# Regions of a routed decoder layer cleared early, filler units in other banks, and identity matmuls in the pauses of the last pairs' chain

## The reference

```python
x = layernorm(x + attention(x))            # 16 heads of 64, Wq, Wkv, Wo, bo
x = layernorm(x + mlstm(x, ctx, ctx))      # 4 heads of 64: decay matrix from gates, running maxima, RMS norm
xn = layernorm(x) * gamma + beta           # 8 experts, hidden 1024, the best 2 for each token
p = softmax(xn @ Wr + br); scores, idx = top_k(p, 2)
y_e = relu(xn @ W1[e] + b1[e]) @ W2[e] + b2[e]
x = layernorm(x + sum_k scores[k] * (y[idx[k]] - c[idx[k]] + sum_e c[e]))   # c[e] = relu(b1[e]) @ W2[e] + b2[e]
```

## Time and profile before

| | us |
|---|---|
| median of 3 runs | 877.47 |
| lowest, highest | 872.62, 878.78 |
| the profiled execution | 873.39 |
| its span, first to last instruction | 871.6 |
| pairs and their units (to about 456) | 456 |
| chain of the last pairs (to the first expert tile at 530) | 74 |
| expert tiles (530 to 811) | 281 |
| tail | 61 |

### The profile page before, as it was taken

The page is one execution under the profiler, slowest core; times in us unless marked ns, Lnnn a source line. Parts: engine busy times, 40 slices in busy tenths (PEclk is TensorE's granted clock), DMA queues, the critical chain, the costliest instruction groups (busy, mean ns, idle before and its releaser), DMA issues.

```text
span 871.6 us, 14654 instructions
## 1 busy us (share of the span) xinstructions
PE 709.3 (81%) x4812; PEld 604.3 (69%) x4813; DVE 467.3 (54%) x1078; ACT 328.4 (38%) x987; POOL 246.4 (28%) x196
## 2 busy tenths in 40 slices
PE   5798989988088988989858415999999999998763
PEld 4687877878077868778656314888888888787421
DVE  4334454843255846558465773555555555555345
ACT  4475666746055746646443201222222222222111
POOL 3100010300311302113034347637227300600473
PEclk9899999989589989899785556999999999999755
DMA  9533333331301001010052015615324411110243
GB/s 312 150 116 115 128 116 116 127 115 37 126 14 37 26 19 55 1 38 25 2 181 66 7 42 175 188 61 164 130 66 156 138 36 42 61 37 19 68 122 113
DMA packets 62507, 77.36 MB, mean 89 GB/s; under 512 B 5836, under 2 KB 54520, under 8 KB 62456
## 3 DMA queue, kind: packets, MB, share of 16 engines
q1 hardware_dynamic: 53832, 47.29, 16.9%
q0 software_dynamic: 8608, 29.37, 10.3%
q10 hardware_dynamic: 16, 0.01, 0.0%
HBM read 45.04 MB, written 31.62 MB: 88 GB/s over the span
## 4 chain that ended last, share of the span: by engine, by line
PE 62%; DVE 11%; ACT 11%; POOL 7%; issue 5%; DMA 4%; POOLq 0%; SPq 0%; DVEq 0%; ACTq 0%
PE bank L919 13%; PE bank L693 7%; PE bank L695 6%; PE bank L694 6%; ACT arena L1026 6%; PE bank L889 4%; PE bank L891 4%; PE bank L890 4%; PE bank L899 4%; POOL arena L683 4%; PE bank L838 3%; PE bank L807 3%; DVE arena L1187 2%; PE bank L771 2%; ACT arena L999 1%
## 5 line engine op out<-in xcount | busy, mean ns | idle before, releaser
L919 PE MATMUL bank<-w_ring,hidT_hi 128*128 x320 | 119.9, 408 | 3.3 <-DVE hidT_lo L1535 3.3
L1026 ACT ACTIVATE arena<-bank,negmx 128x128 f32<-128x128 f32 x256 | 90.7, 373 | 51.7 <-DVE negmx L1179 51.5
L1142 ACT ACTIVATE hidT_hi<-bank 128x512 fp32r<-128x512 f32 x80 | 43.5, 596 | 174.6 <-PE bank L899 174.6
L618 POOL DMA_INDIRECT xg_dram<-arena,slot x32 | 34.2, 1067 | 174.8 <-DVE slot L1378 112.0
L919 PE MATMUL bank<-w_ring,hidT_lo 128*128 x320 | 83.4, 281 | 0.0
L1508 DVE TENSOR_TENSOR arena<-bank,b_rep 128x512 f32<-128x512 f32 x80 | 55.3, 691 | 41.9 <-PE bank L891 41.5
L1185 DVE RECIPROCAL rinv<-rsum 128x8 f32<-128x8 f32 x32 | 6.5, 203 | 127.4 <-ACT arena L1026 127.4
L889 PE MATMUL bank<-w_ring,xgT_hi 128*128 x160 | 67.8, 424 | 4.5 <-DVE xgT_lo L1527 2.7
L919 PEld LDWEIGHTS bank<-w_ring,hidT_hi 128*128 128x128 f32 x320 | 60.1, 188 | 15.0 <-issue 4.0
L1514 DVE TENSOR_REDUCE work<-bank 128x256 f32<-128x512 f32 x40 | 27.7, 691 | 79.5 <-PE bank L919 79.5
L574 POOL TENSOR_TENSOR w_ring<-w_raw,w_ring 128x2048 fp32r<-128x2048 f32 x14 | 64.4, 4597 | 1.2
(11 more groups left out here) (240 smaller groups left out, 1839.7 us busy)
## 6 DMA issues: line engine op xcount, KB each, us to landing
xg_dram<-zeros SPq DMA_DIRECT2D x9, 2176.0 KB, 9.1
w_raw<-in_L_ffn_W_dram POOLq DMA_DIRECT2D x16, 1024.0 KB, 5.8
work<-xg_dram SPq DMA_DIRECT2D x40, 128.0 KB, 2.0
y_dram<-work SPq DMA_DIRECT2D x40, 128.0 KB, 1.7
b_rep<-in_L_ffn_b_dram POOLq DMA_DIRECT2D x8, 512.0 KB, 4.1
work<-gmax_dram SPq DMA_DIRECT2D x14, 256.0 KB, 3.7
arena<-in_x_dram SPq DMA_DIRECT2D x8, 256.0 KB, 2.8
xres<-in_x_dram SPq DMA_DIRECT2D x1, 2048.0 KB, 15.1
```

Source lines behind the costliest of these rows:

```text
L919: last = pe.matmul(o, l, r, start=c == 0 and l is both[0], stop=c == FC - 1 and l is both[0])
L1026: last = nc.scalar.activation(probs[:, n % 2, h * S:(h + 1) * S], ps_score[:, h * S:(h + 1) * S], ACT.Exp, bias=negmx[:, n % 2, h:h + 1], ...
```

## The change

Seven edits.

1. Clears: one a step, at steps 1 to 9 of the loop.
2. Banks in the loop: L, R and G go to bank 7 (between two sequences' output projections), T to banks 4 and 5 (between two transposes). Waits on `wo_read`, `pT_copied` and on the readers of T, G and R keep the owners apart.
3. Order in the loop: T first in step 1, G ahead of two v; R in the second list of step 2; S in the first list of step 3. On ACT, `soft_gates` goes to the start of step 2, `exp_of_m` to its end. On DVE, `weigh` goes ahead of the logits, `choose`, `gate_sums` and `head_sums` ahead of `weights_of`, `find_slots` behind it.
4. Bias 0 is loaded ahead of the weights, bias 1 and 2 later.
5. Expert 0 is rounded on ACT ahead of the copy of N(A), its rests are subtracted on DVE within the chain (`rest_early`).
6. Expert 1 is loaded and rounded within the chain (ACT), its first rest is DVE's there, its second GpSimd's after the last scatter (`rest_of_second`).
7. TensorE runs 6 + 22 + 16 + 30 + 16 identity matmuls ahead of five units of the chain and 40 behind it, into bank 6, which nothing reads.

```diff
-        ps_ring = bank[0:6]
+        ps_ring = [*bank[0:6], bank[7]]
...
             if s == 1:
-                return (of("L", i - 3) + of("X", i - 1) + of("x", i + 1) + of("v", i, 1, 0) + of("T", i - 2),
-                        of("v", i, 0, 1) + of("v", i, 1, 1) + of("G", i - 1))
+                return (of("T", i - 2) + of("L", i - 3) + of("X", i - 1) + of("x", i + 1) + of("v", i, 1, 0),
+                        of("G", i - 1) + of("v", i, 0, 1) + of("v", i, 1, 1))
             if s == 2:
-                return (of("U", i - 2, 0) + of("R", i - 3) + of("q", i + 1, 0) + of("U", i - 2, 1) + of("k", i + 1, 0),
-                        of("q", i + 1, 1) + of("k", i + 1, 1))
-            return (of("v", i + 1, 0, 0) + of("w", i, 0, 0) + of("q", i + 1, 2),
-                    of("w", i, 0, 1) + of("k", i + 1, 2) + of("S", i - 1))
+                return (of("U", i - 2, 0) + of("q", i + 1, 0) + of("U", i - 2, 1) + of("k", i + 1, 0),
+                        of("q", i + 1, 1) + of("R", i - 3) + of("k", i + 1, 1))
+            return (of("v", i + 1, 0, 0) + of("S", i - 1) + of("q", i + 1, 2) + of("w", i, 0, 0),
+                    of("w", i, 0, 1) + of("k", i + 1, 2))
...
+                    if not at_end and un[0] in "TLRG":
+                        ks = (4, 5) if un[0] == "T" else (6,)
+                    else:
+                        ks = [(turn + k) % (6 if at_end else 2) for k in range(2 if un[0] in "TB" else 1)]
+                        turn += len(ks)
...
-                    if s < 2 and 2 * i + s <= E:
-                        done(sp, ("q", i, 3) if s == 0 else ("v", i, 1, 1))
-                        clear_rows(2 * i + s)
+                    if 1 <= STEPS * i + s <= E + 1:
+                        done(sp, {0: ("q", i, 3), 1: ("v", i, 1, 1), 2: ("k", i + 1, 1), 3: ("k", i + 1, 2)}[s])
+                        clear_rows(STEPS * i + s - 1)
...
+            def rest_of_second():
+
+                both = w_ring[:, 1, W_WORDS:2 * W_WORDS].rearrange("p (g k n) -> p g k n", k=2, n=D)
+                pool.wait_ge(w_rounded, 4)
+                pool.tensor_tensor(both[:, :, 1, :], w_raw[:, KC * F:2 * KC * F].rearrange("p (g n) -> p g n", n=D),
+                                   both[:, :, 0, :].bitcast(F32), ALU.subtract).then_inc(w_split, 1)
+                pool.wait_ge(w_split, 4)
+                for part in range(2):
+                    load_raw(2, part)
...
                         done(pool, ("v", Z, 1, 1))
+                        load_bias(0)
                         for part in range(2):
                             load_raw(0, part)
-                        load_bias(0)
-            load_bias(1)
             scale_xn(A)
+            rstd_of_pair(Z)
             for b in range(2):
                 mask(Y, b)
-            rstd_of_pair(Z)
-            load_bias(2)
+            load_bias(1)
             scatter(A)
             head_norm(Y)
+            load_after_first(0)
             for b in range(2):
                 mask(Z, b)
             both_norms(Y)
             scale_xn(Y)
+            load_after_first(1)
             head_norm(Z)
             both_norms(Z)
+            load_bias(2)
             scatter(Y)
             scatter(Z)
+            rest_of_second()
             for part in range(2):
-                split_first(part)
-            for e in range(1, RING):
-                for part in range(2):
-                    split(e, part)
+                split(2, part)
...
-            run(DRAIN)
+            def fill(n):
+
+                for _ in range(n):
+                    pe.matmul(bank[6][:, 0:P], ident[:, :], ident[:, :], start=True, stop=True)
+
+            pauses = {("N", A): 6, ("U", Z, 0): 22, ("R", Y): 16, ("N", Z): 30, ("R", Z): 16}
+            for un in DRAIN:
+                fill(pauses.get(un, 0))
+                run([un])
+            fill(40)
...
+                    if s == 2 and i >= 1:
+                        soft_gates(i - 1)
                     copies(before[:early])
...
-                    if s == 3 and i >= 1:
-                        exp_of_m(i - 1)
...
-                    if s == 2 and i >= 1:
-                        soft_gates(i - 1)
                     copies(after[1:])
+                    if s == 2 and i >= 1:
+                        exp_of_m(i - 1)
...
             copy_unit(("C", Z))
-            copy_unit(("N", A))
             act.wait_ge(wo_done, B)
             for part in range(2):
-                round_first(part)
+                round_early(0, part)
+            copy_unit(("N", A))
             copy_unit(("X", Z))
...
             choice_exp(Y)
+            for part in range(2):
+                round_early(1, part)
             copy_unit(("N", Z))
...
+                    if s == 1 and i >= 2:
+                        weigh(i - 2)
                     if s == 1 and i >= 3:
                         logits_in(i - 3)
                     if s == 1 and i + 1 < PAIRS:
                         rest_x(i + 1)
-                    if s == 1 and i >= 2:
-                        weigh(i - 2)
-                    if s == 2 and i >= 3:
-                        find_slots(i - 3)
+                    if s == 1 and i >= 3:
+                        choose(i - 3)
+                    if s == 2 and i >= 1:
+                        gate_sums(i - 1)
+                    if s == 2 and i >= 2:
+                        head_sums(i - 2)
...
                         weights_of(n + 1)
...
                     if s == 1 and i >= 1:
                         read_gates(i - 1)
-                    if s == 2 and i >= 1:
-                        gate_sums(i - 1)
-                    if s == 2 and i >= 2:
-                        head_sums(i - 2)
+                    if s == 2 and i >= 3:
+                        find_slots(i - 3)
...
             weigh(Y)
+            rest_early(0, 0)
             logits_in(A)
...
             both_norms(Y)
+            rest_early(0, 1)
             head_sums(Z)
...
             both_norms(Z)
+            rest_early(1, 0)
             logits_in(Z)
```

More of the change, by code:

```diff
@@ L272, in decoder_layer @@
         proj_done = sem("proj_done")
-        ring_free = [sem(f"ring_free{k}") for k in range(6)]
+        ring_free = [sem(f"ring_free{k}") for k in range(7)]
         scores_done = sem("scores_done")
@@ L392, in decoder_layer @@
         FIRST = [("x", 0), ("q", 0, 0), ("k", 0, 0), ("q", 0, 1), ("k", 0, 1), ("v", 0, 0, 0)]
-        ordinal, place, uses = {}, {}, [0] * 6
-        for banks_of, units in ((2, FIRST + [un for i in range(PAIRS) for s in range(STEPS) for part in fillers(i, s)
-                                             for un in part]), (6, DRAIN)):
+        ordinal, place, uses = {}, {}, [0] * 7
+        for at_end, units in ((False, FIRST + [un for i in range(PAIRS) for s in range(STEPS) for part in fillers(i, s)
+                                               for un in part]), (True, DRAIN)):
             turn = 0
@@ L399, in decoder_layer @@
                     ordinal[un] = len(ordinal)
[L400 to L404 removed]
+                    if not at_end and un[0] in "TLRG":
[3 more added lines that the diff above has]
+                        turn += len(ks)
+                    place[un] = [(k, uses[k]) for k in ks]
+                    for k in ks:
                         uses[k] += 1
@@ L780, in unit @@
                     read(pe, ("N", p))
+                    if p < A:
+                        pe.wait_ge(wo_read, 2 * (p + 3))
                     for b in range(2):
@@ L816, in out_proj @@
                     pe.wait_ge(wo_read, 2 * i + b)
+                if half == 0 and b == 0:
+                    for un in (("G", i - 1), ("R", i - 3)):
+                        if un in place:
+                            read(pe, un)
                 for c in range(4 * half, 4 * half + 4):
@@ L836, in weights_transposed @@
                     pe.wait_ge(pT_copied, n)
+                if n % STEPS == 1 and n // STEPS >= 2:
+                    read(pe, ("T", n // STEPS - 2))
                 for h in range(8):
@@ L1102, in _ @@
                         choice_exp(i - 3)
+                    copies(after[1:])
                     if s == 2 and i >= 1:
-                        soft_gates(i - 1)
-                    copies(after[1:])
+                        exp_of_m(i - 1)
                     act.wait_ge(oT_done, n + 1)
```

33 lines of the change are left out of this document (15 added, 18 removed).

## The result

The changed kernel takes 844.16 us (median of 4 runs, 843.37 to 845.07) beside 875.05 (872.42 to 878.78) of the kernel before on the same chip: a ratio of 0.9644, with a 95% interval of 0.9599 to 0.969. That is 30.9 us less. I had forecast 830, with a range of 818 to 850, so the range held and the forecast was 14 us too low. The narrower range of the forecast itself, 820 to 838, did not hold.

A forecast was written before the change was run, and what follows sets the result against it. TensorE is busy most of the span; bounds are a long wait rooted in SP's queue order, small bank waits, and half clock before the expert tiles. 873.4 - 22.4 - 9.4 - 15.2 = 826.4, plus 4.1 as median: 830; range 818 to 850.

The forecast's parts named there:

- Part 1: Loop: regions of `xg_dram` cleared early, one a step, so the first scatter no longer waits; gain 22.4 us.
- one wait whose root is SP's queue: Long pair, 76.53 us: TensorE waits for VectorE, VectorE for GpSimd, GpSimd for a ninth clear issued late.
- The store of the gate maxima: Pair 1 step 2, behind a clear on SP's queue: lands some 5 us later; up to 1.5 could show, 0 taken.
- Part 2: Loop's order and banks: waits of x, T and R go, a new one comes; gain 9.4 us, bounds 0 and 15.4.
- the new wait: Pairs 3 to 6: U(1) waits for U(0)'s bank, ACT's copy standing behind `soft_gates`; 4.0 us a pair.
- the longer cold stretch: Pairs 3 to 6, behind the idle TensorE of step 2: half clock for longer, may take 0.5 us a pair.
- the new wait eats part 2: Rival, loop: U(1) behind `soft_gates` and a longer low clock leave the reordering worth 0; 840 us, chance 0.17.
- my upper bound: Most that the loop's new order and banks could bring: 15.4 us.
- Part 3: Last pairs' chain up to the first expert tile: bias first, early rests, fills for the clock; gain 15.2 us.
- 0.9 at L(Y): Last pairs' chain: gain at L(Y) from matmuls sped up by fills that raise the clock, capped by VectorE's rests.
- two rests paid for in full: Chain: by the Skill's rule, rests beside GpSimd would cost 4.5 us in place of the 0.5 taken.
- the first two rivals: Loop reordering worth 0 (840 us, chance 0.17); chain gain halved by rests, roundings and falling clock (838 us, chance 0.15).

The follow-up runs named there:

- c1: Kernel before with only the early clears (one region a step, steps 1 to 9): 852.99 us, ratio 0.9728.
- c2: Changed kernel with the loop's order, banks, ACT and VectorE order of before; early clears, chain and fills stay: 841.30 us, ratio 0.9597.
- c8: Changed kernel with 16 identity matmuls ahead of U(1) in pairs 3 to 7, where TensorE waits: 835.71 us, ratio 0.958.
- c10: c5 with, in addition, ACT's copy of q ahead of the exponentials in step 2: 811.87 us, ratio 0.9302.
- c4: Changed kernel with ACT's `soft_gates` behind the copy of U(0) instead of ahead of it: 845.25 us, ratio 0.9647.
- c5: Changed kernel with VectorE's `choose` moved from ahead of the weights in step 1 to behind the maxima in step 2: 819.41 us, ratio 0.9379.
- c12: Changed kernel with `rest_early(0, 1)` moved ahead of the last logits and `rest_early(1, 0)` behind the last slots, load and rounding moved to match: 849.95 us, ratio 0.9742.
- c3: Changed kernel without any of the 130 identity matmuls: 845.37 us, ratio 0.9654.
- c6: Changed kernel with the fills ahead of U(Z), R(Y), N(Z), R(Z) cut from 22, 16, 30, 16 to 18, 8, 28, 14: 843.47 us, ratio 0.9672.
- c9: Changed kernel with `choose` still in step 1 but behind the softmax weights, as before: 840.14 us, ratio 0.9625.
- c7: Changed kernel with 44 instead of 40 fills ahead of the first expert tile: 840.63 us, ratio 0.963.
- c11: c10 with, in step 3, the second half of the exponentials also ahead of the copy of k: 808.61 us, ratio 0.9256.

## Why the prediction was right or wrong

**Part 1, clears: right.** 22.4 forecast, 22.4 measured (c1). That the two agree to the tenth is luck, as c1's four runs spread over 3.6 us and its trace differs from c2's over the same code by 2.1. The reading that three engines stood in one wait whose root is SP's queue held. The store of the gate maxima that I had let off with 0 cost nothing that c1 shows.

**Part 2, the new wait: right in place, length and size, and still wrong in the sum.** I had worked out U(1)'s start as 20.25 us behind the scores of step 1; it is 301.18 - 280.87 = 20.31. Step 1 was to shrink by 3.3, from 15.73 to 12.4; it takes 12.48. Step 3 gives back 0.9 (12.47 against 11.54), 0.7 forecast. The step that failed is "step 3's scores start 3.0 earlier than today ... the longer cold stretch may take 0.5". They should have stood 29.2 us behind those of step 1; they stand at 31.73. The 8.95 us that I allowed from U(1) to them is what c8 measures with the clock held, 8.87. Behind 4.1 us of idle TensorE the stretch runs at half clock for 6.8 us and takes 11.42. I had written that the clock would fall over the wait and then priced the work behind it as if it had not: 2.5 us a pair in place of 0.5: 2.0 more than the sum allowed, 8 of its 9.4 us over four pairs. Pair 2, for which I had forecast a gain of 1.7, lost 0.9 (48.91 us against 48.03): its step 2 takes 14.39, and 11.70 once q's copy is first (c10), so the wait for q's copy behind the exponentials stands there in small, and the clock fell over it. This is the rival "the new wait eats part 2", to which I had given 0.17.

**What I had not seen: the wait's root.** I laid the wait to `soft_gates` ahead of ACT's copy. c4 took that away and nothing changed, since the maxima and with them the exponentials and q's copy were just as late. My sum had `choose`, the weights and the gates in a row, 12.0 to 18.1, and stopped there; one line further stood the maxima of the next step, on which more engines wait than on the gates. c5 shows what the loop gives once `choose` is out of this place: 23 us on the changed kernel and, by the ratios, 19 on the loop of before (c2), more than the 15.4 of my upper bound. One routine held it back, and it had stood in the same step before the change. Whether the old loop would have gained as much from moving it wasn't tried. So -2.9 is what part 2 is worth with `choose` in step 1; what it is worth with `choose` moved in both loops stays open.

**Part 3, the chain: the places right, the sizes too high.** Its terms, in us behind the scores of pair 7:

| point | before | after | gain | forecast |
|---|---|---|---|---|
| L(A) | 52.56 | 47.18 | 5.4 | 5.5 |
| `head_sums(Z)` | 80.01 | 76.03 | 4.0 | 5.4 |
| N(Z) | 95.32 | 90.44 | 4.9 | 6.3 |
| first scatter of Z | 105.90 | 99.09 | 6.8 | 8.5 |
| end of its last issue | 112.82 | 103.96 | 8.9 | 10.6 |
| first row transposes | 118.93 | 107.88 | 11.1 | 12.9 |
| first Relu | 130.34 | 118.01 | 12.3 | 15.7 |

(The forecast column adds the terms as the prediction did: 5.4; 0.9 at L(Y); 0.7, 0.8 and 0.7 behind N(Z); 2.1, 2.3 and 2.8. The 0.5 off for the rests would come last.) L(A), the last scatter's issue (2.05: 8.86 less 6.81) and the row load (2.2) are as forecast, and behind N(Z) 1.9 of 2.2 came. Two terms failed.

First, "`rest_early(0, 1)` stands ahead of `head_sums(Z)`, where VectorE idled 2.2 us: hidden". The first view has VectorE's three rests: `rest_early(0, 0)`, with nothing of GpSimd beside it, `rest_early(0, 1)` and `rest_early(1, 0)`. The second has what GpSimd ran beside the last two, the third scatter issue among it:

```profile
438.61 2.28 DVE L1422 TENSOR_TENSOR w_ring<-w_raw,w_ring 128x2048 fp32r<-128x2048 f32 x1
...
462.65 3.31 DVE L1422 TENSOR_TENSOR w_ring<-w_raw,w_ring 128x2048 fp32r<-128x2048 f32 x1
...
480.58 2.29 DVE L1422 TENSOR_TENSOR w_ring<-w_raw,w_ring 128x2048 fp32r<-128x2048 f32 x1
```

```profile
462.54 1.26 POOL L618 TENSOR_TENSOR arena<-arena,norms 128x512 f32<-128x512 f32 x1
...
481.07 2.64 POOL L632 DMA_INDIRECT xg_dram<-arena,slot  x1 [0.30 <-issue]
```

A rest alone is 2.28 us and this one 3.31, begun 0.11 behind an instruction of GpSimd that reads SBUF. It outlasted its cover by 1.4, and c12 gave 1.3 of that back. The third rest took 2.29 and was just hidden, ahead of the last logits; GpSimd's issue beside it paid instead, 2.64 us where the other seven of pairs Y and Z take 0.97 to 1.09, off the chain. The rule of the Trainium skill that I had weighed (SBUF — State Buffer, "two separate sides": VectorE with two SBUF inputs and GpSimd reading SBUF exclude each other for a whole instruction) fits these rows: the 1.0 by which the second rest is longer lies within GpSimd's instruction of 1.26. What I had drawn from it, two rests paid for in full, 4.5 us, did not come; 1.4 was paid. The cast of c12 has one input. The same section counts in VectorE's modes that use both ports, and the cast's end with GpSimd's instruction agrees with it; but no run here shows which mode the cast ran in, and it had begun first.

Second, the fills. Their price was right: 30 of them took 6.94 us at full clock (473.50 to 480.44), 0.23 each, and 16 took 6.71 at half clock, 0.42 each. What they were to bring was not. The 0.9 at L(Y) was VectorE's wait for its logits (1.07 before), and that wait is gone because VectorE itself is late: from 462.65 to the last logits it is never idle for over 0.4 us, so nobody waits for a faster matmul, and N(Z) stands where it stands without any fills (90.21 in c3). By c3 the fills bring 1.0 up to the last R (96.87 against 97.89), 0.6 more up to the rows and 1.15 in the first tile, 2.7 in place of 5.9. The tile is the largest miss: 1.3 of 2.8 came, as the clock was low again. Two of the signs that the prediction named didn't come out either: the clock was not near 1.0 from the first long fill on (0.52 from 466 to 473), and fills did run on after what they waited for, which I had called a sign of being wrong; by c6 that cost nothing.

**Behind the first Relu, forecast as untouched: 4.2 us lost** between these two traces. 1.6 is a fall of the clock from 769.6 to 773; 2.6 lies behind the last matmul, where VectorE stood 3.1 us for a queue that the trace doesn't name ("remote"):

```profile
826.84 0.17 DVE L1625 TENSOR_SCALAR ve<-mv 128x4 f32<-128x4 f32 x1 [3.12 <-remote]
```

Both stand in the trace of c1 too, which has nothing of parts 2 and 3 (first Relu to the last tile's last matmul 269.9 where the trace of before has 268.4; start of the last two matmuls to the end 16.9 where it has 14.4). And c9 and c12, which have parts 2 and 3, lack both. So they aren't an effect of the chain or the loop; what they come from wasn't tried.

**The whole.** Forecast in the trace's terms: 22.4 + 9.4 + 15.2 = 47.0 from 873.4. Measured, by kernels: 22.4, -2.9 and 11.7. The profiled run took 843.9 where the sum gave 826.4, 17.5 us more; the forecast of 830 came nearer only by the 4.1 that I had added for the median, of which 0.3 was there. The range held because it had been drawn wide enough for either of the first two rivals. In the runs both came at once, the first in full and the second in part, and the sum of the two still lay inside 850.

## What to carry to other kernels

When a new wait is found in a plan, follow what stands behind it on the engine that is late, not only what waits in front: here the gates were the first victim of `choose` and the maxima, one line further, the dearer one. Price the matmuls behind a wait of some 4 us at half clock (6.8 us of low clock in each of the pairs 3 to 6), or fill the wait; but first ask whether the wait can go, which brought 23 us where filling it brought 6 to 9. Work moved into another engine's idle time must be checked against what runs beside it, on VectorE and GpSimd above all: a rest of 2.29 us took 3.31, and a cast of 0.18 took 5.22.

## What the runs showed of the hardware

- **Fills raise the clock, but don't hold it for certain.** Windows of the changed kernel: four stretches of the chain in which TensorE runs fills most of the time, and the first tile.

```profile
454.00:458.00 4.00, 4.00 (x20) 3.98 (x21) 3.44 (x8) 2.34 (x9) 2.60 (x4) 0.50 0.54 151
458.00:462.00 4.00, 4.00 (x34) 4.00 (x33) 3.83 (x13) 0.00 (x0) 1.94 (x2) 0.87 0.29 117
...
466.00:473.00 7.00, 7.00 (x35) 7.00 (x36) 5.86 (x32) 2.26 (x3) 2.65 (x2) 0.52 0.53 152
473.00:480.00 7.00, 7.00 (x65) 7.00 (x64) 6.14 (x21) 1.64 (x1) 2.93 (x4) 1.00 0.16 61
...
500.00:504.00 4.00, 4.00 (x12) 3.09 (x11) 0.69 (x1) 0.00 (x0) 0.40 (x1) 0.58 0.93 325
```

  The 22 fills raised it midway, as I had assumed, but it fell at 466, after idle times of 0.54 and 0.77 us around N(Y), and stayed low through 7 us of gapless fills.
- **The first tile's clock is not a matter of a few fills.** It was low in the changed kernel, c4, c6 and c7 (10.13 to 10.16 us from row transposes to first Relu) and in c8, c9 and c11 (10.05, 10.03 and 9.86), and full in c2, c5 and c10 (8.55 to 8.58, the forecast 2.8 less than the 11.41 of before). All have the same 40 fills, but for c7, and idle times of 0.9 to 1.2 and 1.33 us ahead of it. c7's four fills more cut the first of these to 0.29 and changed nothing. What decides it stays open.
- **The same wait, two outcomes.** At the end of the expert tiles TensorE waits 2.1 us for `hidT_lo` in every trace. Behind it the clock fell in the changed kernel, c1, c2, c4 to c7, c10 and c11 (269.8 to 270.1 us from the first Relu to the last tile's last matmul) and held in the kernel before, c3, c8, c9 and c12 (268.2 to 268.7). The windows of the changed kernel:

```profile
768.00:770.00 2.00, 1.42 (x7) 1.30 (x8) 1.53 (x3) 0.00 (x0) 0.00 (x0) 0.91 0.00 0
770.00:771.00 1.00, 1.00 (x4) 0.81 (x4) 0.00 (x0) 0.00 (x0) 0.00 (x0) 0.50 0.00 0
```

  So two traces can differ by 1.6 us here with no cause in the kernels that these runs show. VectorE's stall behind the last matmul is as fickle: waits put down to "remote" of 1.6 to 5.3 us near the end stand in the changed kernel, c1 to c5 and c7, and none in the kernel before, c6 and c8 to c12.
